# Rounding the second half of the value weights on VectorE instead of ScalarE, at the head of a decoder layer

## The reference

```python
x = x + attn(layernorm(x))     # qkv = xn @ Wqkv + b; 4 heads' worth of width: q, k, v are 256 wide
x = x + xattn(layernorm(x))    # fake-quantised xn times fake-quantised ctx
x = x + ffn(layernorm(x))      # argmax of 64 picks one hidden unit per block of 3584
```

## Time and profile before

| | |
|---|---|
| median of 3 runs | 770.89 us (770.38 to 771.21) |
| profiled execution, its own time | 770.48 us |
| its span, first to last instruction | 768.6 us |
| time around the span | 1.88 us |
| TensorE busy | 762.0 us, 99% of the span, in 3586 matmuls |
| VectorE, ScalarE, GpSimd busy | 613.8, 247.3 and 468.8 us |
| DMA in the first 20 us | between 232 and 472 GB/s in most slices |
| granted TensorE clock | 1.00 in the stretches read |

### The profile page before, as it was taken

How to read it: one execution, slowest core, us unless ns; L and a number is a source line. 1 busy time by engine, 2 the same in 40 slices (tenths; PEclk the granted TensorE clock), 3 DMA queues, 4 the chain that set the end, 5 groups by cost and what they waited for, 6 DMA issues and landing times.

```text
span 768.6 us, 11457 instructions
## 1 busy us (share of the span) xinstructions
PE 762.0 (99%) x3586; PEld 625.1 (81%) x3586; DVE 613.8 (80%) x974; ACT 247.3 (32%) x378; POOL 468.8 (61%) x306
## 2 busy tenths in 40 slices
PE   8999999999999999999999999999999999999998
PEld 8888887478888888888888888888888888888887
DVE  5888769998887878888878788787888787778864
ACT  6347668884132120303121221203031212222120
POOL 4878898779997264646547363636464563737260
PEclk9999999999999999999999999999999999999999
DMA  9536405300222221222222222212122222222114
GB/s 319 209 109 217 171 6 156 60 15 1 69 68 71 67 70 22 68 73 68 75 68 68 75 68 68 68 53 60 44 68 75 68 75 68 68 68 68 61 38 194
DMA packets 59636, 64.19 MB, mean 84 GB/s; under 512 B 41312, under 2 KB 43616, under 8 KB 59360
## 3 DMA queue, kind: packets, MB, share of 16 engines
q1 hardware_dynamic: 59328, 62.75, 26.0%
q10 hardware_dynamic: 288, 1.18, 0.4%
HBM read 50.79 MB, written 4.19 MB: 72 GB/s over the span
## 4 chain that ended last, share of the span: by engine, by line
PE 92%; DVE 4%; ACT 2%; DMA 1%; issue 1%; SPq 0%; DVEq 0%; ACTq 0%
PE bank L1911 13%; PE bank L1912 13%; PE bank L1913 13%; PE bank L1811 12%; PE bank L1812 12%; PE bank L1813 12%; PE bank L1618 4%; PE bank L1620 4%; PE bank L1619 4%; PE bank L1802 2%; DMA x<-x_in 1%; DVE x L1302 1%; PE bank L1781 1%; DVE xn L1289 1%; ACT spread L775 1%
## 5 line engine op out<-in xcount | busy, mean ns | idle before, releaser
L1911 PE MATMUL bank<-w_hi,h_hi 128*128 128x512 f32 (+1 forms) x450 | 175.5, 390 | 0.0
L1912 PE MATMUL bank<-w_lo,h_hi 128*128 128x512 f32 (+1 forms) x450 | 175.3, 390 | 0.0
L1913 PE MATMUL bank<-w_hi,h_lo 128*128 128x512 f32 (+1 forms) x450 | 174.7, 388 | 0.0
L1415 DVE TENSOR_TENSOR x<-bank,x 128x512 f32<-128x512 f32 x207 | 132.7, 683 | 48.2 <-PE bank L1913 48.2
L638 POOL TENSOR_TENSOR lo_r<-r,slot 128x512 fp32r<-128x512 f32 x54 | 70.9, 1314 | 158.0 <-ACT slot L882 158.0
L1913 PEld LDWEIGHTS bank<-w_hi,h_lo 128*128 128x128 f32 x450 | 84.5, 188 | 18.0
L1911 PEld LDWEIGHTS bank<-w_hi,h_hi 128*128 128x128 f32 x450 | 84.5, 188 | 17.3 <-POOL w_lo L643 0.3
L1912 PEld LDWEIGHTS bank<-w_lo,h_hi 128*128 128x128 f32 x450 | 84.7, 188 | 15.0
L1811 PE MATMUL bank<-xT_hi,slot 128*128 128x512 f32 x232 | 90.5, 390 | 0.0
L1812 PE MATMUL bank<-xT_lo,slot 128*128 128x512 f32 x232 | 90.3, 389 | 0.0
L946 ACT ACTIVATE h_hi<-bank 128x512 fp32r<-128x512 f32 x56 | 33.4, 600 | 118.9 <-DVE bank L1356 81.4
(11 more groups left out here) (212 smaller groups left out, 1595.0 us busy)
## 6 DMA issues: line engine op xcount, KB each, us to landing
r<-w SPq DMA_DIRECT2D x56, 256.0 KB, 3.4
w_raw<-w SPq DMA_DIRECT2D x28, 512.0 KB, 4.0
x<-x_in SPq DMA_DIRECT2D x8, 512.0 KB, 10.7
ctx_raw<-ctx_in SPq DMA_DIRECT2D x8, 512.0 KB, 3.5
xn<-ctx_in SPq DMA_DIRECT2D x8, 512.0 KB, 4.5
out<-x SPq DMA_DIRECT2D x7, 512.0 KB, 2.6
W_raw<-wqkv SPq DMA_DIRECT2D x6, 512.0 KB, 10.9
xT_raw<-xT_in SPq DMA_DIRECT2D x1, 2048.0 KB, 19.7
```

The source lines that it names most:

```text
L1415: nc.vector.tensor_tensor(x[:, t, c], bank[unit_banks(g)[p]][:, :], x[:, t, c], ALU.add).then_inc(unit_added, 1)
L1911: nc.tensor.matmul(dst, h_hi[:, j, m], w2_hi[:, j, c], start=j == 0, stop=False)
L1912: nc.tensor.matmul(dst, h_hi[:, j, m], w2_lo[:, j, c], start=False, stop=False)
L1913: last = nc.tensor.matmul(dst, h_lo[:, j, m], w2_hi[:, j, c], start=False, stop=j == GJ - 1)
```

## The change

VectorE rounds both halves of the value weights, one directly behind the other, each after its own load; ScalarE's rounding of half 1, between its copies of tiles 0 and 1, goes. TensorE and GpSimd wait for the same event under the other semaphore, and the counts that GpSimd expects of ScalarE fall by one.

```diff
@@ gpsimd
             for n, i in enumerate(W_ORDER):
                 for h in range(2):
-                    if (n, h) == (0, 0):
-                        pool.wait_ge(V_hi_done, 1)
+                    if n == 0:
+                        pool.wait_ge(V_hi_done, h + 1)
                     else:
-                        pool.wait_ge(W_hi_done, 2 * n + h)
+                        pool.wait_ge(W_hi_done, 2 * n + h - 1)
@@ scalar
             both(hi_T, 0, 0)
-            hi_W(W_ORDER[0], 1)
             both(hi_T, 0, 1)
@@ vector
             norm_scale(0, 0)
             norm_scale(0, 1)
-            dve.wait_ge(W_loaded[W_ORDER[0]][0], 16)
-            nc.vector.tensor_copy(W_hi[:, W_ORDER[0], 0:KD // 2, :],
-                                  W_raw[:, W_ORDER[0], 0:KD // 2, :]).then_inc(V_hi_done, 1)
+            for h in range(2):
+                k = slice(h * KD // 2, (h + 1) * KD // 2)
+                dve.wait_ge(W_loaded[W_ORDER[0]][h], 16)
+                nc.vector.tensor_copy(W_hi[:, W_ORDER[0], k, :], W_raw[:, W_ORDER[0], k, :]).then_inc(V_hi_done, 1)
             first_stats(2)
@@ tensor, first_values
                         if s == 0 and k == KD // 2:
-                            pe.wait_ge(W_hi_done, 1)
+                            pe.wait_ge(V_hi_done, 2)
```

## The result

| kernel | runs | median | lowest to highest |
|---|---|---|---|
| before | 22 | 770.81 us | 770.13 to 771.53 |
| changed | 22 | 772.66 us | 769.91 to 773.30 |

What follows compares the result with a forecast made beforehand. The prediction took the head's chain from tile 2's load through VectorE's statistics to bound what the change can touch. A 1.46 us delay from the held CAST, with 0 for ScalarE, added to 770.89 gave 772.35 us; range 770.5 to 773.0.

Steps and rivals of the forecast that it cites:

- The bound and the hole: Head: VectorE delays between 11.03 and 16.09 us reach the end one to one; the new rounding enters VectorE's 1.49 us idle.
- The two ways: Head: VectorE's second CAST and GpSimd's first subtraction, 0.08 us apart, dispute a port; cost 1.46 us or zero.
- GpSimd first: Head: subtraction begins before the second CAST, holding it to 12.58 us; statistics of tile 2 1.46 us later; chance 0.63.
- the CAST first: Rival, head: half 1 lands before about 9.62 us, GpSimd starts later, time unchanged at 770.9 us; chance 0.23.
- runs that go both ways: Rival: some executions go one way, some the other; median 770.9 to 772.4 us; chance 0.07.
- The likeliest case: GpSimd's subtraction starts before the second CAST; median 772.35 us, alone 772.0 to 772.8; chance 0.63.
- The price of the held CAST: VectorE, head: CAST held to 12.03 us, ends 0.55 us later at 12.58; tile 2's statistics 1.46 us later.
- The clock: Rival: TensorE's clock falls behind a new hole, doubling 3.65 us of work; 5.1 us slower, 776.0 us; chance 0.04.
- a hole of 1.1 us near 17.7 us: TensorE, head: stands idle about 1.1 us after tile 0's low-by-high products, before tile 2 can be turned.
- The sum: Whole kernel: 1.46 us delay added to the median of 770.89 gives 772.35 us, 0.19% longer.
- Nothing for ScalarE and the later GpSimd: Head: ScalarE's freed 1.05 us rounding gains 0 at the end; GpSimd's later subtraction is ready before TensorE asks.

Runs made afterwards that it cites:

- e3_pool_later: Changed kernel, with GpSimd's first subtraction waiting for both VectorE CASTs instead of the first alone; median 770.39 us, ratio 0.9999 to the kernel before.
- e4_one_source: Changed kernel, with VectorE's second CAST written as a maximum over groups of one element; median 770.67 us, ratio 1.0000 to the kernel before.
- e6_delay: Kernel before, with VectorE's statistics of tile 2 held until GpSimd's first subtraction is done; median 771.50 us, ratio 1.0016.
- e8_x2_first: Kernel before, with tile 2's load ahead of half 1's load in SyncE's queue; median 770.22 us, ratio 1.0000.
- e1_repeat: Changed kernel run again with no edit, 11 runs; median 772.34 us, ratio 1.0016 to the kernel before.
- e2_held: Changed kernel, with VectorE's second CAST also waiting until TensorE has turned the first half of tile 0; median 772.91 us, ratio 1.0025 to the kernel before.
- e5_fill: e2_held plus unread turnings of the identity filling TensorE's holes before half 1 and tile 1's product; median 772.27 us, ratio 1.0023 to the kernel before.
- e7_split: e2_held, with GpSimd's first subtraction in two instructions of 512 columns each; median 771.05 us, ratio 1.0010 to the kernel before.

## Why the prediction was right, and where it was not

**The bound and the hole.** Right for a delay. The statistics of tile 2 set the pace, and a delay of them reaches the end. For four profiled executions with the clock at 1.000 all the way, the start of those statistics against 11.05 us and the time against 770.48 us are: changed, -0.39 and -0.40; e3_pool_later, -0.40 and -0.36; e4_one_source, +0.53 and +0.45; e6_delay, +1.06 and +1.03. A start that is earlier still pays only in part: e8_x2_first has -1.15 and -0.33. The start of tile 3's first value product, 23.79 us before, follows the time in all of these to 0.1 us, and in e1_repeat too, with its fall of the clock: 25.95, +2.16, for a time of +2.13. The three kernels with the added wait of e2_held are dearer than that: +2.19 and +2.42 for e2_held, +1.60 and +1.86 for e5_fill, +0.27 and +0.74 for e7_split. In these three the waits of TensorE's weight loads for the turned activations (line 1761 of before), much later in the kernel, are 2.0 us in the trace instead of 1.6 or 1.7. Why is open.

**The two ways.** Right in kind: GpSimd first, or the CAST first, by 0.08 us in the profile read. I gave 0.63, 0.23 and 0.07 for runs that go both ways. The last is what happened: 18 of 22 runs are in the upper groups, 4 in the lower one, and e1_repeat has 9 and 2. Where the CAST is first, GpSimd lost 0.37 us, less than the 0.55 I gave it. The chances of single executions were about right, but I should have given them to executions and not to the kernel. The likeliest case's time still stands for the median, since four in five go that way.

**The price of the held CAST.** Right. I took 12.58 for its end and 0.55 for the tail (the time from GpSimd's end to the CAST's); e1_repeat shows 12.43 and 0.55, with a GpSimd that began 0.14 us sooner. In the six runs of the changed kernel that were held at clock 1.000, the median is (772.27 + 772.36) / 2 = 772.32, 1.51 us above that of before; 1.46 was forecast.

**The clock.** This is the mis-sized term. I priced a fall at 3.65 us with a chance of 0.04, for a hole of 1.1 us near 17.7 us. It fell in 12 of 22 runs, and the median of those, (772.89 + 772.92) / 2 = 772.91, is 0.59 us above the held ones at full clock. The same difference of medians is 0.80 in e1_repeat, 0.81 in e2_held and 0.86 in e6_delay, so the price is 0.6 to 0.9 us. Two things were wrong. The hole is an earlier one: I had TensorE go on with tile 1's products directly behind half 1, and overlooked that they take the bank that lo_T of tile 0 frees, behind the very statistics that I had just delayed by 1.46 us. And the price was set as if TensorE's doubled work of 20 to 24 us were all on the path. The slow work, 0.75 us more for 8 products and 0.81 for 16, lies in a stretch in which TensorE would otherwise have waited for VectorE, so a part of it is covered: with statistics 1.30 us late, tile 3's first product is 2.16 us late, so 0.86 of the 1.56 us got through. The predicted hole at 17.7 us never came: in e1_repeat TensorE was late itself, and in e5_fill it worked until 18.9 and turned tile 2 at 19.02.

**The sum.** 772.35 forecast, 772.66 measured, 0.3 us apart. The difference of the median is the clock: 12 of 22 runs have it, and the median lies at the border of the two held groups. That it still lies within the 772.0 to 772.8 of the likeliest case is owed to the small price of this fall, which I didn't foresee, and not to the sum. The CAST-first runs pull the ratio down to 1.0017; e2_held, which has none, has 1.0025.

**Nothing for ScalarE and the later GpSimd.** Right for the two together, by e3_pool_later at 0.9999.

## What to carry to other kernels

Before you move a copy onto VectorE, look at what GpSimd runs at that moment, and above all at what the copy before it releases: here the first of two copies started the very instruction that shut out the second. Release GpSimd behind the last of them (e3_pool_later), cut its instruction in two (e7_split, which still lost 0.6 us), or use a form of copy that isn't held (e4_one_source). And when a trace leaves an order to a tenth of a microsecond, expect both orders among the executions and look at every run, not at the median.

## What the runs showed of the hardware that was not expected

- A load's landing moves by up to a microsecond between executions of kernels that issue the same loads in the same order: half 1, issued at 2.13 us, landed 7.2 us later in two of the profiles, 7.5, 7.6 (before), 7.8, 7.9 and 7.9 us later in five, and 8.2 in two. GpSimd's start, which hangs on the first CAST, lies between 9.51 and 9.84 us in the nine profiles in which the first CAST releases it. The two together decide the race.
- The held kernels' clock fell in some executions and not in others: 12 of 18, 5 of 9 and 5 of 8 in the changed kernel, e1_repeat and e2_held, 2 of 11 in e6_delay, none of 9 in e5_fill. A long hole alone doesn't bring it down each time: the profiles of e6_delay and e4_one_source have one of 1.07 and 1.15 us before tile 1's products and a clock of 1.00. And one of the 30 runs of the kernel before beside the first set has 0.998 too, at 772.50 us; no trace shows why. In both traces in which it fell, the 44 turnings of the identity with which TensorE begins had also gone faster (6.41 us in e1_repeat, below, against 7.80 in the profile of before), so that TensorE had stood still 1.26 or 1.33 us before 9.2 us too; in the traces in which it stayed, that early hole was 0.79 us or less, except 1.06 in e3_pool_later, where no long hole follows. Whether this early hole matters was not tried.

```profile
1.54 6.41 PE L1920 MATMUL bank<-id_f 128*128 128x128 f32 x44 [1.54 <-POOL id_f L535]
9.21 0.33 PE L1634 MATMUL bank<-id_f,xn 128*128 128x128 f32 x1 [1.26 <-ACT xn L790]
```
